# Cross attention on one core: projected output with 100 moving columns, query copies on ScalarE

## The reference

```
q = (x @ Wq + bq), k = (ctx @ Wk + bk), v = (ctx @ Wv + bv)   # each [.., 16, 64]
attn = softmax(q k^T / sqrt(64))                              # over the 1444 keys
out  = (attn v).reshape(.., 1024) @ Wo + bo
y = x + out;  result = (y - mean) / sqrt(var + 1e-5) * gamma + beta
```

## Time and profile before

| | us |
|---|---|
| median of 3 runs | 874.84 |
| lowest and highest | 874.22, 880.41 |
| profiled execution | 876.33 |
| its span, first to last instruction | 874.4 |

### The profile page before, as it was taken

The page is one execution under the profiler, slowest core; times in us unless marked ns, Lnnn a source line. Parts: engine busy times, 40 slices in busy tenths (PEclk is TensorE's granted clock), DMA queues, the critical chain, the costliest instruction groups (busy, mean ns, idle before and its releaser), DMA issues.

```text
span 874.4 us, 19571 instructions
## 1 busy us (share of the span) xinstructions
PE 856.8 (98%) x7312; PEld 618.2 (71%) x7312; DVE 797.1 (91%) x998; ACT 756.6 (87%) x1059; POOL 479.6 (55%) x514
## 2 busy tenths in 40 slices
PE   8999999999999999999999999999999999999997
PEld 7577776766677677777677777677777767777675
DVE  4899989899998999989899998999999899999984
ACT  4899898988889898898988889898988989988983
POOL 2153883459746573754647466473755657376210
PEclk7999999999999999999999999999999999999999
DMA  8899999999999999999999999999999999999985
GB/s 192 175 221 192 194 198 184 219 210 206 207 224 200 221 207 227 218 212 218 203 210 225 214 200 221 213 224 208 214 222 215 211 220 202 228 191 207 207 181 127
DMA packets 683938, 180.80 MB, mean 207 GB/s; under 512 B 654596, under 2 KB 683076, under 8 KB 683844
## 3 DMA queue, kind: packets, MB, share of 16 engines
q1 hardware_dynamic: 682372, 179.01, 105.0%
q10 hardware_dynamic: 1344, 0.53, 0.2%
q0 software_dynamic: 128, 0.01, 0.0%
HBM read 15.35 MB, written 0.82 MB: 18 GB/s over the span
## 4 chain that ended last, share of the span: by engine, by line
PE 46%; DVE 26%; ACT 11%; issue 9%; DMA 5%; SPq 3%; ACTq 0%; POOLq 0%; DVEq 0%; POOL 0%
PE ps L662 21%; PE ps L623 19%; DVE p_lo L920 11%; DVE nmax L905 10%; ACT p L1069 6%; DMA pt_hi<-p_hi 4%; ACT p_hi L1077 3%; PE ps L481 2%; PE ps L473 2%; DVE rsum L911 1%; ACT unused L1020 1%; SPq L422 1%; DVE rinv L913 1%; PE ps L488 1%; SPq L413 1%
## 5 line engine op out<-in xcount | busy, mean ns | idle before, releaser
L920 DVE SCALAR_TENSOR_TENSOR p_lo<-p,rinv,p_hi 128x1444 f16<-128x1444 f32 x200 | 362.5, 1813 | 2.3 <-ACT p_hi L1077 1.6
L1077 ACT ACTIVATE p_hi<-p,rinv 128x1444 f16<-128x1444 f32 x200 | 299.8, 1499 | 46.7 <-DVE rinv L913 45.8
L905 DVE TENSOR_REDUCE nmax<-ps 128x1 f32<-128x1446 f32 x200 | 329.8, 1649 | 9.1 <-PE ps L623 8.9
L1069 ACT ACTIVATE p<-ps,nmax 128x1446 f32<-128x1446 f32 x200 | 291.8, 1459 | 29.8 <-DVE nmax L905 28.1
L662 PE MATMUL ps<-pt_hi,c_hi 128*128 128x256 f16 (+1 forms) x1232 | 252.9, 261 | 5.7 <-DMA pt_hi<-p_hi 3.5
L662 PE MATMUL ps<-pt_hi,c_lo 128*128 128x256 f16 (+1 forms) x1232 | 252.9, 261 | 0.0
L623 PE MATMUL ps<-ct_hi,g_hi 128*128 128x482 f16 (+3 forms) x624 | 155.5, 367 | 0.0
L623 PE MATMUL ps<-ct_hi,g_lo 128*128 128x482 f16 (+3 forms) x624 | 154.9, 366 | 0.0
L623 PE MATMUL ps<-ct_lo,g_hi 128*128 128x482 f16 (+3 forms) x624 | 154.9, 366 | 0.0
L662 PEld LDWEIGHTS ps<-pt_hi,c_hi 128*128 128x128 f16 x1232 | 114.2, 98 | 43.0 <-issue 9.6
L662 PE MATMUL ps<-pt_lo,c_hi 128*128 128x256 f16 (+1 forms) x1232 | 138.7, 261 | 0.0
(11 more groups left out here) (134 smaller groups left out, 778.5 us busy)
## 6 DMA issues: line engine op xcount, KB each, us to landing
c_raw<-in_ctx_dram SPq DMA_DIRECT2D x32, 256.0 KB, 6.2
pt_hi<-p_hi SPq DMA_TRANSPOSE x200, 3.5
pt_lo<-p_lo SPq DMA_TRANSPOSE x200, 3.6
c_raw<-in_ctx_dram SPq DMA_DIRECT2D x16, 192.0 KB
c_raw<-in_ctx_dram SPq DMA_DIRECT2D x48, 18.0 KB
out_dram<-late_sb SPq DMA_DIRECT2D x16, 50.0 KB
x_sb<-in_x_dram SPq DMA_DIRECT2D x1, 600.0 KB
o_t<-in_L_xattn_Wq_dram SPq DMA_DIRECT2D x2, 256.0 KB, 4.4
```

Source lines behind the costliest of these rows:

```text
L905: dve.tensor_reduce(nmax[:, n % RING:n % RING + 1], ps[:, bank:bank + 3, 0:KEYW], AX.XY, ALU.max, negate=True).then_inc(s_nm, 1)
L920: dve.scalar_tensor_tensor(out=p_lo[:, n % LOS, 0:KL], in0=p32[:, n % P32S, 0:KL], scalar=rinv[:, i:i + 1], in1=p_hi[:, par, 0:KL], op0=AL ...
L1069: act.activation(p32[:, n % P32S, :].rearrange("p (k w) -> p k w", w=KEYW), ps[:, bank:bank + 3, 0:KEYW], ACT.Exp, bias=nmax[:, i:i + 1], ...
L1077: act.activation(p_hi[:, par, 0:KL], p32[:, n % P32S, 0:KL], ACT.Copy, scale=rinv[:, i:i + 1]).then_inc(s_hi, 1)
```

## The change

- Output projection in parts (L481, batches 2 to 14): M's parts become the stationary side and the rows the moving one. A matmul moves 100 columns instead of 128 and the result comes out transposed, 128 columns of the output by 100 rows. ScalarE copies it with its scale to SBUF (`columns_out`, at r = 9), TensorE transposes it back in float32 at r = 10, and VectorE's `take_rows` follows at r = 10 instead of 9, now a plain addition. The spread of the context maximum and its scale move from r = 10 to 11.
- Queries (batches 1 to 15): `take_queries` moves from VectorE to ScalarE, between `hi_tail` and `hi_part`, and only scales. GpSimd adds the bias in `split_queries` ahead of the split.
- The sums of magnitudes of M move from tiles 24 and 25 to 11 and 12, its total from 27 to 17, its scale from tile 35 to 23, the casts of its high part from 36 to 39 to 24 to 27, and `leave_m_lo` from window 3 to window 2.
- Partition maxima (`c_top`, `ax_max`, `m_max`) and the scaled identities become bfloat16, so that the spreads are matmuls of two-byte operands.

```diff
-    TOP_AT = 10
-    TOP_AT_FIRST = 11
+    BACK_AT = 10
+    TOP_AT = 11
...
-        ident_part = sb("ident_part", [P, 2, P])
+        ident_part = sb("ident_part", [P, 3, P], BF16)
...
-        M_SUM_AT = (24, 25)
-        M_TOTAL_AT = 27
-        MTOP_AT = IN_PAIR + TOP_AT
+        M_SUM_AT = (11, 12)
+        M_TOTAL_AT = 17
+        MTOP_AT = MIXED + TOP_AT
...
-                        mm = pe.matmul(bank[0:QL, 0:D], o16[:, i, rows], m16[:, h, j, :], start=(h == 0 and i == j),
+                        mm = pe.matmul(bank[:, 0:QL], m16[:, h, j, :], o16[:, i, rows], start=(h == 0 and i == j),
                                        stop=(h == H - 1 and j == 1))
...
-                pe.matmul(bank[:, 0:P], spread(c_max[:, NT + 1:NT + 2]), ident_part[:, min(b, 1), :], start=True, stop=True).then_inc(s_top, 1)
+                pe.matmul(bank[:, 2 * P:3 * P], spread(c_top[:, :]), ident_part[:, min(b, 1), :], start=True, stop=True).then_inc(s_top, 1)
...
+                if r == BACK_AT and w > 0 and in_parts(w - 1):
+                    pe.wait_ge(s_of, w - FIRST_PARTS)
+                    pe.transpose(bank[0:QL, P:2 * P], out_t[:, (w - 1) % 2, :], ident[:, :]).then_inc(s_bk, 1)
...
-            def take_queries(b, g):
-                dve.wait_ge(s_gj, NG * (b - 1) + g + 1)
-                dve.wait_ge(s_gsc, b + 1)
-                dve.wait_ge(s_gs, NG * (b - 1) + g)
-                copy_queries(b, g, ps[:, JOB_BANK, :]).then_inc(s_gv, 1)
...
-                if in_parts(b):
-                    dve.wait_ge(s_fu, b - FIRST_PARTS + 1)
-                    dve.scalar_tensor_tensor(out=z[:, par, :], in0=ps[0:QL, JOB_BANK, 0:D], scalar=fin_un[0:QL, par:par + 1],
-                                             in1=x_sb[:, b, :], op0=ALU.mult, op1=ALU.add).then_inc(s_z, 1)
-                else:
-                    dve.tensor_tensor(z[:, par, :], ps[0:QL, JOB_BANK, 0:D], x_sb[:, b, :], ALU.add).then_inc(s_z, 1)
+                dve.tensor_tensor(z[:, par, :], ps[0:QL, JOB_BANK, at:at + D], x_sb[:, b, :], ALU.add).then_inc(s_z, 1)
...
+            def take_queries(b, g):
+                by = unscale[:, b % UNSCALES:b % UNSCALES + 1] if b < 3 else g_un_b[:, b % 2:b % 2 + 1]
+                act.wait_ge(s_gj, NG * (b - 1) + g + 1)
+                act.wait_ge(s_gsc, b + 1)
+                act.wait_ge(s_gs, NG * (b - 1) + g)
+                act.activation(g_raw[:, HG * g:HG * g + HG, :], split(ps[:, JOB_BANK, :], HG, QL), ACT.Copy,
+                               scale=by).then_inc(s_gv, 1)
+
+            def columns_out(b):
+                act.wait_ge(s_fin, b + 1)
+                act.wait_ge(s_fu, b - FIRST_PARTS + 1)
+                act.activation(out_t[:, b % 2, :], ps[:, JOB_BANK, 0:QL], ACT.Copy,
+                               scale=fin_un[:, b % 2:b % 2 + 1]).then_inc(s_of, 1)
...
+                if 0 <= g < NG and w + 1 < B:
+                    take_queries(w + 1, g)
+                if r == ROWS_AT and w > 0 and in_parts(w - 1):
+                    columns_out(w - 1)
                 hi_part(n)
...
                 pool.wait_ge(s_gv, NG * (b - 1) + g + 1)
+                heads = slice(HG * g, HG * g + HG)
+                pool.tensor_tensor(g_raw[:, heads, :], g_raw[:, heads, :],
+                                   gb_b[:, par, heads].unsqueeze(2).to_broadcast([P, HG, QL]), ALU.add).then_inc(s_bi, 1)
+                pool.wait_ge(s_bi, NG * (b - 1) + g + 1)
...
-                    if w == FIRST_PARTS + 1:
+                    if w == FIRST_PARTS:
                         leave_m_lo(g)
```

More of the change, by code:

```diff
@@ L10 @@
 F16 = mybir.dt.float16
+BF16 = mybir.dt.bfloat16
 P = 128
@@ L193, in cross_attention_kernel @@
         c_tail = sb("c_tail", [P, 2, D], F16)
-        unused = sb("unused", [P, KT // SUMS * D + 256], mybir.dt.bfloat16)
-        c_max = sb("c_max", [P, NT + 2])
+        unused = sb("unused", [P, KT // SUMS * D + 256], BF16)
+        c_max = sb("c_max", [P, NT + 1])
+        c_top = sb("c_top", [P, 1], BF16)
         c_scaled = sb("c_scaled", [P, TG * D])
@@ L359, in split @@
             return bank[:, 0:n * w].rearrange("p (n w) -> p n w", w=w)
+        es.enter_context(nc.allow_low_precision(reason="sums of magnitudes set a scale that cancels; none may exceed it by much"))
         block = es.enter_context(nc.Block())
@@ L695, in job @@
                         pe.wait_ge(s_us, b + 1)
+                    if g == 0 and b == window(MTOP_AT)[0] + 2:
+                        pe.wait_ge(s_ma, 1)
                     if b < 3:
@@ L730, in job @@
                         pe.wait_ge(s_mc, 1)
-                        pe.matmul(bank[:, P:2 * P], spread(m_max[:, :]), ident[:, :], start=True, stop=True).then_inc(s_mt, 1)
+                        pe.matmul(bank[:, 3 * P:4 * P], spread(m_max[:, :]), ident_part[:, 2, :], start=True, stop=True).then_inc(s_mt, 1)
                     spread_context_max(bank, w + 2)
@@ L886, in parts_scale @@
                 dve.wait_ge(s_axt, 1)
-                dve.tensor_reduce(ax_top[:, :], split(ps[:, JOB_BANK, P:], 2, P), AX.X, ALU.max).then_inc(s_axa, 1)
+                dve.tensor_reduce(ax_top[:, :], split(ps[:, JOB_BANK, :], 2, P), AX.X, ALU.max).then_inc(s_axa, 1)
                 dve.wait_ge(s_axa, 1)
@@ L968, in _ @@
                 row_inverse(n)
-                if r == ROWS_AT and w > 0:
+                if w > 0 and r == (BACK_AT if in_parts(w - 1) else ROWS_AT):
                     take_rows(w - 1)
@@ L1116, in _ @@
                     continue
+                w, r = window(n)
+                g = r - (G_AT if w else G_AT_FIRST)
+                if 0 <= g < NG and w + 1 < B:
+                    take_queries(w + 1, g)
+                if r == ROWS_AT and w > 0 and in_parts(w - 1):
+                    columns_out(w - 1)
                 hi_part(n)
-                w, r = window(n)
                 if r in CHI_AT and w + 1 < B:
@@ L1158, in _ @@
             pool.wait_ge(s_ident, 1)
-            for i, top in enumerate((C_RANGE, C_SUM_RANGE)):
+            for i, top in enumerate((C_RANGE, C_SUM_RANGE, 1.0)):
                 pool.tensor_scalar(ident_part[:, i, :], ident[:, :], 1.0 / top, 1.0, ALU.mult, ALU.mult).then_inc(s_part_id, 1)
```

44 lines of the change are left out of this document (25 added, 19 removed).

## The result

The changed kernel takes 871.18 us (median of 20 runs, 868.25 to 874.66) against 874.85 for the kernel before, run beside it on the same chip (20 runs, 871.60 to 880.41). The medians are 3.7 us apart. The ratio over the rounds is 0.9953, with a 95% interval of 0.9939 to 0.9967, which is 4.1 us (2.9 to 5.3). The forecast was 9.6 us less, and a median of 865.2 us.

A forecast was written before the change was run, and what follows sets the result against it. TensorE's work was taken to set the steady-state period. 7.6 us of its work (6.8 - 2.1 + 2.9) plus 2.0 of stall made 9.6 us off, 874.84 to 865.2 us; range 861 to 872, forecast case 862 to 868.5 at 0.60.

The forecast's parts named there:

- the forecast's 7.6: TensorE's work: 6.8 us off by the narrow output projection, 2.1 added by turning back, 2.9 off by two-byte spreads.
- the narrow side brings nothing: Rival at the output projection: the weight load sets the pace, so the 6.8 us are lost, 872 us; chance 0.03.
- under 53.5 was the sign: Sign of being right: window 3 under 53.5 us, no idle TensorE ahead of its first output projection.
- 102.6 was the sign: Sign of being right: windows 10 and 11 together in about 102.6 us, where they took 103.6.
- costed both at nothing: Query copies on ScalarE counted as 0; for the narrow side, no loss beside the old weight split was counted.
- the 50 named as the sign of the rival: Sign that ScalarE sets the pace: VectorE's waits for exponentials over 50 us, against 31.8 before.
- its work sets the period: Steady state: TensorE's work sums to 102.8 of 103.6 us in windows 10 and 11, leaving under 1% unused.
- The gap: ScalarE's 0.2 us wait between small tail and large cast, plus 0.65 after the cast, to hide the query copy.
- ScalarE takes over: Rival at r = 6 to 9: ScalarE needs 4.0 to 4.6 us a step, 6.8 us lost, 872 us; chance 0.19.
- up to 1 us either way: Windows 0 and 1: two ScalarE sums enter, four casts leave its first steps' exchange; counted as nothing, within 1 us.
- GpSimd (10%): Rival at r = 1 to 5: GpSimd lengthens VectorE's large subtraction to about 2.4 us or more; 886 us, chance 0.10.
- More than the sum: Rival: 0.8 us idle per window pair and window 2's waits go too, 4 to 5 us more, 860.5; chance 0.08.

## Why the prediction was right in direction and too large

**Right, on TensorE.** Its busy time behind the head fell by 7.3 us of the forecast's 7.6. Twelve output matmuls take 0.54 us, as forecast. The transpose costs 0.10 us on TensorE's path (bound: 0.165) and the spread 0.06. Timeline, TensorE, window 11:

```profile
640.49 0.27 PE L736 MATMUL ps<-ident,out_t 128*100 128x128 f32 x1
640.59 0.78 PE L631 MATMUL ps<-ct_hi,g_hi 128*128 128x482 f16 x3
...
644.40 0.22 PE L554 MATMUL ps<-ident_part,c_top 128*128 128x128 bf16 x1
644.46 0.78 PE L631 MATMUL ps<-ct_hi,g_hi 128*128 128x482 f16 x3
```

No wait stands ahead of the transpose: the copy is in time. The rival that the narrow side brings nothing falls. Of the two rules that the Trainium skill gives in "TensorE: Matmul & The Clock Gate", section Back-to-back issue gap, the one for a matmul by itself makes 44.2 ns of 100 columns. The trace agrees with it though every matmul here has a weight load: 0.54/12 = 45 ns.

**Right, on the sooner weights.** Window 3 lost 2.0 us of the 2.5 forecast for it, to 53.7 where under 53.5 was the sign, and has no idle time ahead of its first output projection. Windows 10 and 11 take 102.9 us where 102.6 was the sign. What was missed is that the other two parts would have made this stall 5 to 8 us: the copies through GpSimd's longer row of work, which the trace shows; the narrow side most likely through the later scale, which no run took apart. The prediction had costed both at nothing and did not ask what they do beside the old split. It did not need to for this kernel, but a reader who took the change apart by its terms would have got the sign of each part wrong.

**Right, in the steady state, on ScalarE and GpSimd.** The copies alone leave windows 4 to 13 at 516.5 us (517.9 before), ScalarE's extra work hidden. VectorE waits 18.3 us for scores in place of 8.9; its waits for exponentials are 37.2 us, under the 50 named as the sign of the rival. VectorE is busy 89%, not 87: the large subtraction is 0.04 us longer, 8.4 us in 200, and the copies, whose records overlap with their neighbours', free some 7 us less than their own length. For this the prediction weighed the Trainium skill's "SBUF — State Buffer", section SBUF: two separate sides, by which one of the two engines waits for the whole instruction of the other. The trace agrees in kind: 39 of GpSimd's 60 additions take 0.85 us and 21 about 2.3. But leaving them out brings nothing.

**Wrong: "its work sets the period" taken as "each microsecond off its work is one off the time".** The step of the sum that failed is 7.6 us of TensorE's work at full value. The work did go (7.3 us), but behind the head TensorE's idle time rose from 8.9 to 13.7 us although 2.0 of stall went with the sooner weights. So in this execution 6.8 us came back as other waiting, 5.5 of them for transposes (3.5 before, 9.0 after). That next limit was not priced, and the prediction read neither the row of these waits nor the DMA column of the earlier trace rows (1.16 and 1.09 in windows 10 and 11). In odd windows a faster TensorE comes to the transposes of r = 4 earlier, and beside the context's loads these do not land earlier. Without loads the full 5.2 us of windows 4 to 13 appear, with them 0.7 in the profiled execution and 3.0 to 5.1 in its sisters, three of which have their loads a step sooner. By the ratios this is 6.6 - 4.1 = 2.5 us, of 5.5 that were missing. That the loads' bytes are what delays the changed kernel is shown: by leaving the loads out, by leaving out most of their bytes, and by moving them without gain. The size of 2.5 us is not: by the intervals it could be anything from nothing to about 6.

**Wrong: the first windows and the last.** Without loads the trace gives 7.3 us from first maximum to end, not 9.6. Window 0 is 1.0 us longer where 0.2 less was forecast: ScalarE's copies there lie beside casts and sums, not in a gap. The gap was read from window 11 and carried to a window whose engine has other work; the forecast's own rival "ScalarE takes over" (3.4 us plus 0.6 plus 0.9) was right, but in window 0 only. Shown by the copies alone (+1.0) and by taking them back (50.92, and 50.8 with all copies on VectorE). Window 1 is 0.4 longer, from the exchange of sums and casts, inside the "up to 1 us either way"; with the weights late it is 58.23, with them sooner 58.5. The last window with the end is 0.6 us longer for 0.4 less. The other kernels with the narrow side show it too (66.95 to 67.97 us, against 66.74 to 66.81 without), and what causes it was not settled. Windows 2 and 14 gained 1.3 us more than forecast together, which no run took apart.

**The rivals.** GpSimd (10%) is refuted. "More than the sum" (8%) did not come: an idle that the prediction hoped to see vanish grew, since it was waiting for DMAs. The measured 871.2 lies inside the range of 861 to 872, but by luck: it lies at what "ScalarE takes over" and "the narrow side brings nothing" gave, 872, yet neither mechanism is its cause. A time that fits a rival is no proof of it: the waits of the changed kernel point to the transposes, and neither rival speaks of these.

## What to carry to other kernels

Before work taken off the busiest engine is booked at full value, ask what it waits for already, however little, DMAs among it: here 3.5 us of waiting for transposes became 9.0, and the loads beside them took, by the middle of wide intervals, over a third of the gain. Read the gap that shall hide a moved instruction in every kind of window, not in the quiet one. And test parts both with and without the rest: here each of two parts alone made the kernel slower, and their sum was faster only because a third part had moved a deadline.

## What the runs showed of the hardware

- A DMA transpose of probabilities holds SyncE's queue for 1.4 us in the median; 38 of 400 hold it for more than 2 us, up to 3.3, and 25 still do without any context load (up to 2.9). With loads of a quarter to a third of the bytes in the same places, TensorE's waits for transposes were 3.8 us, where full loads have 4.5 to 9.5.
- After 4.9, 5.7 and 7.9 us of idleness TensorE ran at its lower clock: three score matmuls took 1.41 us for 0.78. Behind the 2.00 us of the earlier trace rows they took 0.78, at a granted clock of 1.00.
- In the head TensorE ran at its lower clock from 12 us for about 10 us in one profiled execution and for about 3 in another, whose first row maximum came 2.1 us sooner: two single traces are best compared from behind it.
- A four-byte transpose of 128 by 100 costs TensorE 0.10 us between other matmuls, and a two-byte spread 0.06 where the four-byte one took 0.22.
